# Graph attention plus gated update: the first table built between adjacency halves, and the start-up transfers split over two queues

## What is computed

```
h = relu(layernorm(x))
# layer 1, graph attention with 4 heads of 32
wh = h @ weight;  lp = wh . a_src;  lc = wh . a_dst          # per head
e[i,j] = leaky_relu(lp[i] + lc[j], 0.2) where adj[i,j] > 0, else -9e15
x = x + softmax_j(e) @ wh
# layer 2, messages and a gated cell
h = relu(layernorm(x));  agg = adj @ h
msg = relu(agg @ W_msg.T + b_msg)
x = x + gru_cell(msg, h, W_ih, W_hh, b_ih, b_hh)
```

## Time and profile before

| what | us |
|---|---|
| runs | 1160.31, 1157.52, 1160.41 |
| median | 1160.31 |
| profiled execution | 1159.31 |
| its span | 1157.6 |
| TensorE busy | 679.1 (59%) |
| VectorE busy | 586.4 (51%) |
| ScalarE busy | 686.2 (59%) |
| GpSimd busy | 592.6 (51%) |
| SP's queue, share of the 16 DMA engines | 58.8% |

### The profile page before, as it was taken

How to read it: one execution, slowest core, us unless ns; L and a number is a source line. 1 busy time by engine, 2 the same in 40 slices (tenths; PEclk the granted TensorE clock), 3 DMA queues, 4 the chain that set the end, 5 groups by cost and what they waited for, 6 DMA issues and landing times. The chain is left out here.

```text
span 1157.6 us, 14697 instructions
## 1 busy us (share of the span) xinstructions
PE 679.1 (59%) x4141; PEld 523.0 (45%) x4141; DVE 586.4 (51%) x2487; ACT 686.2 (59%) x723; POOL 592.6 (51%) x598
## 2 busy tenths in 40 slices
PE   0076555765665566566566566655332776777774
PEld 0064334554454454354354444444331565555563
DVE  4632524656656646747647647557331244433443
ACT  0497866886887887788778778772210333233331
POOL 0021074464564654654744744735705777777770
PEclk9997887888788788778878878876555989899998
DMA  7748999999999999999999999951101222222220
GB/s 237 308 149 306 428 401 413 412 411 416 393 396 413 390 413 407 389 406 405 393 413 403 392 413 398 388 224 20 42 5 44 60 67 68 57 68 70 67 66 25
DMA packets 58623, 311.92 MB, mean 269 GB/s; under 512 B 15577, under 2 KB 32994, under 8 KB 42210
## 3 DMA queue, kind: packets, MB, share of 16 engines
q1 hardware_dynamic: 30434, 277.37, 58.8%
q0 software_dynamic: 19712, 30.02, 10.7%
q10 hardware_dynamic: 8448, 4.20, 1.2%
HBM read 298.82 MB, written 12.71 MB: 269 GB/s over the span
## 5 line engine op out<-in xcount | busy, mean ns | idle before, releaser
L457 ACT ACTIVATE ind<-adj_in 128x4144 bf16<-128x4144 int32 (+1 forms) x128 | 461.9, 3609 | 39.1 <-DMA adj_in<-in_adj 22.8
L397 POOL DMA_INDIRECT rows_in<-wh_table,idx x192 | 198.2, 1032 | 304.4 <-DVE val_idx L869 250.7
L602 PE MATMUL ps<-ind,bit_w 128*128 128x296 bf16 (+1 forms) x1792 | 312.2, 340 | 0.0
L602 PEld LDWEIGHTS ps<-ind,bit_w 128*128 128x128 bf16 x1792 | 206.9, 115 | 89.9
L1030 POOL DMA_INDIRECT rows_in<-g_table,idx x192 | 197.6, 1029 | 91.3 <-issue 54.0
L401 POOL DMA_INDIRECT vals_in<-in_adj,val_idx x192 | 183.6, 956 | 58.6 <-issue 58.6
L799 DVE MAX8 cand<-ps 128x8 f32<-128x148 f32 x256 | 61.9, 304 | 117.6 <-PE ps L602 117.2
L598 PE MATMUL ps<-idx_r,idx_w 128*128 128x296 bf16 x128 | 44.2, 346 | 129.8 <-ACT ind L457 129.6
L1164 DVE TENSOR_SCALAR ownT<-iota,edge_row 128x128 f32<-128x128 f32 x64 | 14.7, 324 | 152.6 <-DMA rows_in<-g_table,idx 152.5
L598 PEld LDWEIGHTS ps<-idx_r,idx_w 128*128 128x128 bf16 x128 | 15.8, 123 | 140.4 <-ACT ind L457 126.5
L619 PE MATMUL ps<-rest,tri 128*128 128x4 f32 x32 | 9.0, 352 | 115.0 <-DVE rest L833 115.0
(11 more groups left out here) (220 smaller groups left out, 1514.7 us busy)
## 6 DMA issues: line engine op xcount, KB each, us to landing
adj_in<-in_adj SPq DMA_DIRECT2D x64, 2072.0 KB, 15.0
adj_in<-in_adj SPq DMA_DIRECT2D x64, 2024.0 KB, 14.0
wh_table<-t_buf POOLq DMA_DIRECT2D x16, 264.0 KB, 3.0
g_table<-t_buf ACTq DMA_DIRECT2D x16, 256.0 KB, 25.1
out<-adj_in SPq DMA_DIRECT2D x16, 256.0 KB, 2.3
rows_in<-wh_table,idx POOLq DMA_INDIRECT x192, 6.7
vals_in<-in_adj,val_idx POOLq DMA_INDIRECT x192, 6.7
rows_in<-g_table,idx POOLq DMA_INDIRECT x192, 2.8
```

The lines of the kernel that those rows point to most:

```text
L397: nc.gpsimd.indirect_dma_start(out=rows_in[:, par, t, k, :], out_offset=None, in_=wh_table, in_offset=bass.IndirectOffsetOnAxis(ap=idx[:, ...
L457: nc.scalar.activation(ind[:, t % 2, a:b], adj_in[:, slot, 0:b - a].bitcast(I32), ACT.Relu, bias=1.0, scale=-1.0, accum_out=empty[:, bass. ...
L602: ins = nc.tensor.matmul(o[:, 0:w], bit_w[:, b, :], ind[:, t % 2, c0:c0 + w], start=False, stop=(b == BITS - 1))
```

## The change

- **Queues.** x and the weights move from SP's queue to ScalarE's: weights first, then x in four parts of 16 row tiles (`XC`), each with a semaphore of its own. SP starts with the attention pieces and biases (the biases on a semaphore `b_in` of their own) and goes on to the adjacency.
- **Statistics.** VectorE takes them in four parts (`variance0`, `norm0`); ScalarE's square roots (`deviation0`) stand before recodes 0 (two of them), 1 and 2.
- **The table.** Its units are woven between the halves of steps 0 and 1: `units(m)` gives none for m = 0 and 1, two units a half for m = 2 to 7, one for m = 8 to 11. VectorE now makes the normalised blocks (`rows0`, without the relu), and ScalarE's copy to `hT` takes the relu. `project` has one pair of banks, 5 and 6, so `project(q)` waits for `table(q - 1)`. The blocks lie in `h2` and `attn`.
- **Packs.** `pack` takes the matmuls of a half as soon as that half is recoded; the sum of matmuls is the same.
- **Moved.** The mean row is made at m = 11 and 12, and the biases' rows and `whbar` after the search of m = 11, ahead of `edge_indices` of step 1.

```diff
-W_DMAS = 4 + 2 * H + 9
+W_DMAS = 4 + 2 * H
+B_DMAS = 9
+XC = 16
...
-        h_buf = rows_in[:, :, :, 0, 0:D]
+        h_buf = (h2, attn)
...
+        def units(m):
+            if 2 <= m < 2 * G:
+                return (2 * m - 4, 2 * m - 3)
+            if 2 * G <= m < 3 * G:
+                return (m + G,)
+            return ()
+
+        def turn_bank(q):
+            return 4 if q % 2 and q < 3 * G else 7
...
-                sp.dma_start(x1[:], x_rows).then_inc(x_in, 16)
-                sp.dma_start(wx[:, 0:D], weight).then_inc(w_in, 16)
...
                 sp.wait_ge(const_done, 1)
                 for h in range(H):
                     rows = slice(h * F, (h + 1) * F)
...
-                    sp.dma_start(b_raw[r:r + 1, 0:3 * D], b_ih.rearrange("(o d) -> o d", o=1)).then_inc(w_in, 16)
...
+                    sp.dma_start(b_raw[r:r + 1, 0:3 * D], b_ih.rearrange("(o d) -> o d", o=1)).then_inc(b_in, 16)
+                    sp.dma_start(b_raw[r:r + 1, 3 * D:6 * D], b_hh.rearrange("(o d) -> o d", o=1)).then_inc(b_in, 16)
+                    sp.dma_start(b_all[r:r + 1, 4 * D:5 * D], b_msg.rearrange("(o d) -> o d", o=1)).then_inc(b_in, 16)
                 for n in range(SLOTS):
                     load(n // 2, n % 2, n)
...
+                act.dma_start(wx[:, 0:D], weight).then_inc(w_in, 16)
+                act.dma_start(w_raw[:, 0, :], W_msg).then_inc(w_in, 16)
+                act.dma_start(w_raw[:, 1:4, :], W_ih.rearrange("(c p) d -> p c d", p=P)).then_inc(w_in, 16)
+                act.dma_start(w_raw[:, 4:7, :], W_hh.rearrange("(c p) d -> p c d", p=P)).then_inc(w_in, 16)
+                for c in range(T // XC):
+                    act.dma_start(x1[:, c * XC:(c + 1) * XC, :], x_rows[:, c * XC:(c + 1) * XC, :]).then_inc(x_in[c], 16)
+
+                def deviation0(c):
+                    act.wait_ge(var_done, c + 1)
+                    nc.scalar.activation(sd0[:, c * XC:(c + 1) * XC], var0[:, c * XC:(c + 1) * XC], ACT.Sqrt, bias=epsc[:, 0:1]) \
+                        .then_inc(sd_done, 1)
+
+                def turned0(q):
                     act.wait_ge(htr_done, q + 1)
-                    if not isinstance(q, int) or q >= 2:
+                    if q >= 2:
                         act.wait_ge(wh_done, q - 1)
-                    nc.scalar.activation(hT[:, par].rearrange("p g d -> p (g d)"), ps[:, (7, 4)[par], :], ACT.Identity,
-                                         accum_out=hsum[:, bass.ds(q, 1)]).then_inc(hT_done, 1)
...
+                    def scan(t, half):
+                        indicate(s, t, half)
+                        if isinstance(s, int) and s < 2:
+                            m = s * 2 * G + 2 * t + half
+                            if 2 + m < T // XC:
+                                deviation0(2 + m)
+                            for q in units(m):
+                                turned0(q)
+
+                    if isinstance(s, int) and s == 0:
+                        deviation0(0)
+                        deviation0(1)
+                    if "c" in do:
+                        scan(0, 0)
+                        scan(0, 1)
+                        scan(1, 0)
...
-                def turn0(q, par):
+                def turn0(q):
                     pe.wait_ge(h_done, q + 1)
-                    if not isinstance(q, int) or q >= 2:
-                        pe.wait_ge(hT_done, q - 1)
-                    for t in range(G):
-                        ins = nc.tensor.transpose(ps[:, (7, 4)[par], t * P:(t + 1) * P], h_buf[:, par, t, :], ident[:])
+                    if q >= 1:
+                        pe.wait_ge(hT_done, q if turn_bank(q - 1) == turn_bank(q) else q - 1)
+                    for t in range(G):
+                        ins = nc.tensor.transpose(ps[:, turn_bank(q), t * P:(t + 1) * P], h_buf[q % 2][:, t, :], ident[:])
                     ins.then_inc(htr_done, 1)
 
-                def project(q, par):
+                def project(q):
                     pe.wait_ge(hT_done, q + 1)
-                    if not isinstance(q, int) or q >= 2:
-                        pe.wait_ge(table_rows, q - 1)
-                    for t in range(G):
-                        ins = nc.tensor.matmul(ps[:, (5, 2)[par] + t // 2, (t % 2) * (TW + H):(t % 2 + 1) * (TW + H)], hT[:, par, t, :], wx[:],
+                    if q >= 1:
+                        pe.wait_ge(table_rows, q)
+                    for t in range(G):
+                        ins = nc.tensor.matmul(ps[:, 5 + t // 2, (t % 2) * (TW + H):(t % 2 + 1) * (TW + H)], hT[:, q % 2, t, :], wx[:],
                                                start=True, stop=True)
                     ins.then_inc(wh_done, 1)
...
                 def pack(s, t):
                     tile = s * G + t
-                    pe.wait_ge(ind_done, tile * 2 + 2)
-                    if not isinstance(tile, int) or tile >= 2:
-                        pe.wait_ge(seg_done, tile - 1)
-                    for u in range(2):
-                        o = ps[:, (t % 2) * 2 + u, 0:HALF]
-                        nc.tensor.matmul(o, idx_w[:], idx_r[:, u * HALF:(u + 1) * HALF], start=True, stop=False)
-                        for b in range(BITS):
-                            c0 = b * WORDS + u * HALF
-                            w = min(HALF, N - c0)
-                            ins = nc.tensor.matmul(o[:, 0:w], bit_w[:, b, :], ind[:, t % 2, c0:c0 + w],
-                                                   start=False, stop=(b == BITS - 1))
-                    ins.then_inc(pack_done, 1)
+                    for half in range(2):
+                        pe.wait_ge(ind_done, tile * 2 + half + 1)
+                        if half == 0 and (not isinstance(tile, int) or tile >= 2):
+                            pe.wait_ge(seg_done, tile - 1)
+                        for u in range(2):
+                            o = ps[:, (t % 2) * 2 + u, 0:HALF]
+                            if half == 0:
+                                nc.tensor.matmul(o, idx_w[:], idx_r[:, u * HALF:(u + 1) * HALF], start=True, stop=False)
+                            for b in range(half * (BITS // 2), (half + 1) * (BITS // 2)):
+                                c0 = b * WORDS + u * HALF
+                                w = min(HALF, N - c0)
+                                ins = nc.tensor.matmul(o[:, 0:w], bit_w[:, b, :], ind[:, t % 2, c0:c0 + w],
+                                                       start=False, stop=(b == BITS - 1))
+                        if half:
+                            ins.then_inc(pack_done, 1)
+                        if isinstance(s, int) and s < 2:
+                            m = tile * 2 + half
+                            for q in units(m):
+                                project(q)
+                            for q in units(m + 1):
+                                turn0(q)
+                            if m == 3 * G:
+                                mean_row()
...
+                def variance0(c):
+                    dve.wait_ge(x_in[c], 16)
+                    for t in range(c * XC, (c + 1) * XC):
+                        ins = V.bn_stats(st0[:, t, :], x1[:, t, :])
+                    link(ins)
+                    st = st0[:, c * XC:(c + 1) * XC, :]
+                    mean, half, var = columns_of(mean0, c), columns_of(half0, c), columns_of(var0, c)
+                    V.tensor_tensor(half, st[:, :, 1], st[:, :, 4], ALU.subtract)
+                    V.tensor_tensor(mean, st[:, :, 1], st[:, :, 4], ALU.add)
+                    link(V.tensor_tensor(var, st[:, :, 2], st[:, :, 5], ALU.add))
+                    link(V.scalar_tensor_tensor(out=half, in0=half, scalar=0.25, in1=half, op0=ALU.mult, op1=ALU.mult))
+                    V.scalar_tensor_tensor(out=var, in0=var, scalar=1.0 / D, in1=half, op0=ALU.mult, op1=ALU.add).then_inc(var_done, 1)
+
+                def norm0(c):
+                    dve.wait_ge(sd_done, c + 1)
+                    link(V.reciprocal(columns_of(rs0, c), columns_of(sd0, c)))
+                    link(V.scalar_tensor_tensor(out=columns_of(nmr0, c), in0=columns_of(mean0, c), scalar=-0.5, in1=columns_of(rs0, c),
+                                                op0=ALU.mult, op1=ALU.mult))
+
+                def rows0(q):
+                    if q >= 2:
+                        dve.wait_ge(htr_done, q - 1)
+                    for t in range(G):
+                        n = q * G + t
+                        ins = V.tensor_scalar(h_buf[q % 2][:, t, :], x1[:, n, :], rs0[:, n:n + 1], nmr0[:, n:n + 1], ALU.mult, ALU.add)
+                    ins.then_inc(h_done, 1)
...
+                def table(q):
+                    dve.wait_ge(wh_done, q + 1)
+                    if q >= 2:
+                        dve.wait_ge(table_out[q % 2], (q // 2) * 16)
...
                 link(V.memset(hbar_b[:], 1.0 / N))
-                link(V.tensor_tensor(mean0[:], st0[:, :, 1], st0[:, :, 4], ALU.add))
```

(40 more changed lines are left out.)

146 lines of the change are left out of this document (48 added, 98 removed).

## The result

The changed kernel takes 1172.49 us (median of 4 runs, 1169.82 to 1176.59), the kernel before 1160.18 in the same comparison: a ratio of 1.011 (95% interval 1.0085 to 1.0135), 12 us slower where 7 us faster was forecast. The profiled execution took 1170.57 us with a span of 1168.9.

The account below looks back on a forecast made before the run. The prediction took the scan to be bound by transfers, nearly all adjacency. Recode 19 would come 9 us ahead, later gathers give back 3, leaving 6: 1159.31 - 6 = 1153.3, taken as 1153 us, range 1143 to 1163.

Parts of the forecast that it names:

- a gain of 6 us: Whole kernel: recode 19 comes 9 us ahead, group 0's later gathers give back 3 us, 6 us remain.
- The scan is bound by transfers: Scan, 120 to 760 us: DMA engines busy for 1.01 of the time at 404 GB/s, no other engine reaching 0.8.
- The ceiling of 32 us: Before 120 us: DMA engines idle 35 us, about 2.5 remain in any kernel, so 32 us at most can be gained.
- What the change moves: Whole kernel: bytes unchanged, engines' work hardly changed, normalised blocks go to VectorE; order changes, with the table's waits between halves.
- The rival that ended slower: The low-clock rival on halves 2 to 11: 1163 us with a fifth of TensorE's work at low level; chance 0.25.
- x's parts at 32, 36, 40: Start: adjacency loads hold back x, parts 1 to 3 land at about 32, 36 and 40 us; recode 2 ends at 56.
- x comes first: Rival, start: x lands by 20 to 26 us, recode 2 ends at about 40; gain 13 us, 1146 us; chance 0.26.
- the main case: The forecast itself, whole kernel: 6 us gained, 1153 us; chance 0.43.
- Halves 2 to 7 at 9.2 us: Steps 0 and 1, two table units a half: one line on TensorE and VectorE takes 9.2 us, six halves 55 us.
- TensorE at its low level: Rival, halves 2 to 11: a fifth of TensorE's work at 1.2 GHz adds 9.6 us, 1163 us; chance 0.25.
- `recv` at 142, recode 19 at 164: End of the woven table: ScalarE passes its copy of `recv` at 142 us; recode 19 at about 164 instead of 172.87.
- What the profile would show: Mechanism wrong if the scan's DMA share fell under 1 after 180 us, or if layer 2 changed its length.

Follow-up runs that it names:

- e2_split: The kernel before with the pack split in halves in every step and nothing else: 1135.1 us, ratio 0.981.
- e9_after64: The changed kernel with 64 one-element memsets on VectorE ahead of its wait for x's part 2, shifting its loop: 1145.8 us, ratio 0.989.
- e11_whole64: The changed kernel with the whole pack from step 2 on and 64 one-element memsets on VectorE: 1171.9 us, ratio 1.011.
- e14_split28: The kernel before with the split pack and 28 one-element memsets on VectorE ahead of its wait for the weights: 1166.3 us, ratio 1.005.
- e5_shift28: The kernel before with 28 one-element memsets on VectorE ahead of its wait for the weights: 1168.8 us, ratio 1.009.
- e1_whole: The changed kernel with the whole pack put back from step 2 of the scan on: 1174.0 us, ratio 1.014.
- e3_xfirst: The changed kernel with SyncE waiting for all of x before the first adjacency load: 1158.3 us, ratio 1.001.
- e10_x64: The changed kernel with SyncE waiting for all of x before the first adjacency load, and 64 one-element memsets on VectorE: 1129.3 us, ratio 0.974.

## Why the prediction was wrong

Two steps of the prediction failed. It took the scan's pace for that of the transfers, and so put at nothing both the split pack and the place of VectorE's code; they are worth 22 us and cost 27. And it made the woven table a gain of 6 us where it costs some 10: it had the halves 9.2 us apart, and they came 10.4 apart.

The sum of the difference, from runs: the split pack gives 22 us (e2_split); the woven table with its queues, compared with the block table at the same pack and with the loop in place, **costs** 11 (e9_after64 against e2_split, 1145.8 and 1135.1; 9 by the median of 1144.4); VectorE's reloads cost 27 (after against e9_after64; 28 by the same). -22.5 + 10.7 + 26.7 is 14.9, the distance of after's 1172.5 from the 1157.6 of before in e2_split's comparison (12.3 from the 1160.2 of its own); the forecast was -7. The terms aren't independent, so the sum holds in this order alone. With the loop in place the split pack is worth 22 us (e2_split against before) and 26 (e9_after64 against e11_whole64), with reloads 2.5 (e14_split28 against e5_shift28) and 1.5 (after against e1_whole): a reload takes back nearly all that the split pack gives.

Point by point:

- *The scan is bound by transfers.* **Wrong.** It was read from a DMA share of 1.01 at 404 GB/s. The share is 1.01 at 415 as well (e2_split). The scan of the kernel before was paced by a ring of waits of 44.4 us a step; the 1.07 us that recode 15 waits for its load are one of few. So the split pack had a value of 22 us, with the loop in place, that the sum didn't hold.
- *The ceiling of 32 us* held only for the time before 120 us, where 11 us of it were won (24 us idle instead of 35). They went again behind it. The stretch 120:150 of before, then of after:

```profile
120.00:150.00 30.00, 18.50 (x108) 12.51 (x106) 15.34 (x86) 23.46 (x15) 3.61 (x4) 0.83 1.01 428
```

```profile
120.00:150.00 30.00, 16.65 (x97) 12.81 (x96) 15.56 (x75) 13.88 (x14) 3.01 (x4) 0.78 0.80 271
```

  The chain still paces the halves there, and at 271 instead of 428 GB/s it gives back some 11 us of transfers.
- *What the change moves.* The steps listed instructions, waits, DMAs and queues, and left out where code lies. This is the term that turned the sign. The rival that ended slower had another mechanism.
- *x's parts at 32, 36, 40.* Part 1 came at once (its statistics followed part 0's at 15.17 us), parts 2 and 3 at 36.9 and 45.5 behind waits of 13.8 and 4.2. Recode 2 ended at 53.4 instead of 56: compensating errors, so partly luck. The rival "x comes first" was right for half of x. Made whole (e3_xfirst) it is worth 14 us to after; it had forecast 7 beyond the main case. Its price is there too: over the 16 units `table` waits 25 us for stores with x first and 0.6 in after. The copy's group (count, busy, mean ns, idle before by releaser) up to 150 us, e10_x64, then after:

```profile
L783 DVE COPY parent<-ps 128x16 f32<-128x16 f32 x16 | 2.8, 174 | 53.0 <-PE ps L573 27.7 <-DMA wh_table<-t_buf 25.3
```

```profile
L780 DVE COPY parent<-ps 128x16 f32<-128x16 f32 x16 | 2.8, 175 | 55.0 <-PE ps L570 54.4 <-DMA wh_table<-t_buf 0.6
```

- *Halves 2 to 7 at 9.2 us.* They came 10.4 apart. This is the mis-sized term of the early part: half a pack at the low level of the clock, 3.56 us where I took 1.89, with a granted clock of 0.74 from 50 to 90 us. One half of after:

```profile
86.60 3.56 PE L592 MATMUL ps<-ind,bit_w 128*128 128x296 bf16 x14
...
89.97 1.14 PE L570 MATMUL ps<-wx,hT 128*128 128x136 f32 x8
...
92.16 1.17 PE L570 MATMUL ps<-wx,hT 128*128 128x136 f32 x8 [1.05 <-DVE t_buf L782]
...
94.15 1.11 DVE L772 TENSOR_SCALAR h<-x,rs,nmr 128x128 f32<-128x128 f32 x4
...
95.31 0.66 PE L562 MATMUL ps<-ident,h 128*128 128x128 f32 x4 [1.99 <-DVE h L772]
```

  The chain is the one forecast, link for link; the blocks take 1.1 us for four, not 0.9, and 1.7 go to the clock. The rival "TensorE at its low level" was therefore right in its mechanism: 6 x 1.2 = 7 us, from the point it named, with the granted clock under 0.9 as it had said, if not with halves 11 us apart. The prediction misread its rows here, and gave this rival too little with 0.25: it put TensorE's share of 0.60 between those of the table's stretch and of the scan, but by the earlier trace rows the scan's own share is 388 of 640, or 0.61.
- *`recv` at 142, recode 19 at 164.* 150.5 and 175.4. Halves 2 to 7 took some 63 us where 55 were forecast, less the 2.6 at the start, and halves 8 to 11 some 3 more than the 31 forecast; recode 15 ended at 161.5, and load 19 landed 14 us behind it instead of 10. `child_logits` came at 196.7 instead of 187.
- *What the profile would show.* "Wrong on the mechanism if the scan's DMA share fell under 1 after 180 us": it fell to 0.99 over 120 to 760. The line asked the right question of a column that can't answer it; the GB/s beside it can.

## What to carry to other kernels

A busy share of 1 on the DMA engines doesn't prove that transfers are the bound: look for recodes that wait for loads, and for steps that repeat almost exactly, which are a ring of waits. Waits for loads are no proof either, since a late recode makes its next load late: from 400 to 750 us ScalarE waits 66 us for loads in after and 42 in e9_after64, the faster one. Where a long loop nearly fills what an engine keeps of its code, any edit ahead of it can move it across a block: count the packets of the instruction queue in the loop's stretch, before believing in any cause in the edit itself, and shift the loop by some idle instructions to test it. And start the small transfer that everything waits for ahead of the flood, also at the cost of an idle bus: 11 us of delay for the first load gave 14 us at the end.
